# A graph-attention layer with gathers on GpSimd: every fourth gather waits until the last four have landed

## The reference

```python
Q, K, V = h @ Wq, h @ Wk, h @ Wv                      # 8 heads of 32
score = einsum(K[src], Q[dst]) / sqrt(32) + edge_bias # per edge and head
ex    = exp(score - segment_max(score, dst)[dst])
attn  = ex / segment_sum(ex, dst)[dst]
out   = segment_sum(attn * V[src], dst)               # then @ Wp + bp
```

## Time and profile before

| | |
|---|---|
| median of 3 runs (lowest to highest) | 5461.48 us (5446.13 to 5467.12) |
| the profiled execution: its time, its span | 5467.72 us, 5465.8 us |
| TensorE's mean granted clock over the span | 0.840 |
| busy: PE, DVE, ACT, POOL | 72%, 56%, 34%, 45% |
| first graph's edge pass, from its first gather to its last message product | 238.5 to 1899.0 us |
| in that pass, 238 to 1905 us: busy PE, DVE, ACT, POOL | 1180, 1288, 613, 964 us of 1667 |
| the same: granted clock, DMA engines' busy share, traffic | 0.86, 0.50, 142 GB/s |

### The profile page before, as it was taken

How to read it: one execution, slowest core, us unless ns; L and a number is a source line. 1 busy time by engine, 2 the same in 40 slices (tenths; PEclk the granted TensorE clock), 3 DMA queues, 4 the chain that set the end, 5 groups by cost and what they waited for, 6 DMA issues and landing times. The chain is left out here.

```text
span 5465.8 us, 69110 instructions
## 1 busy us (share of the span) xinstructions
PE 3936.6 (72%) x16154; PEld 2869.7 (53%) x16282; DVE 3067.4 (56%) x7623; ACT 1863.3 (34%) x5073; POOL 2451.9 (45%) x2442
## 2 busy tenths in 40 slices
PE   6867777767777659966953666666666328999999
PEld 4545545555555448866732444444444226777776
DVE  3277778877778775662063666666667773111111
ACT  1333333333333313311222444444445322333332
POOL 2256566666556360000166666666663321333332
PEclk8978888888888879987986767777777559999999
DMA  2545555555555332221173333333332360111111
GB/s 83 185 135 147 142 148 148 147 149 148 142 147 144 89 109 86 94 64 38 44 254 91 93 92 94 94 92 90 91 94 57 113 204 18 33 31 31 31 32 27
DMA packets 316126, 553.64 MB, mean 101 GB/s; under 512 B 63430, under 2 KB 213782, under 8 KB 315856
## 3 DMA queue, kind: packets, MB, share of 16 engines
q0 software_dynamic: 137120, 388.63, 26.6%
q1 hardware_dynamic: 178736, 161.98, 9.6%
HBM read 459.75 MB, written 90.62 MB: 101 GB/s over the span
## 5 line engine op out<-in xcount | busy, mean ns | idle before, releaser
L427 POOL DMA_INDIRECT attend_ring<-kv_rows,all_step_src x880 | 855.5, 972 | 669.8 <-PE attend_ps_agg L468 415.6
L927 POOL DMA_INDIRECT edge_ring<-head_rows,all_step_src x880 | 871.5, 990 | 485.9 <-issue 213.5
L963 PE MATMUL edge_ps_agg<-edge_msg,edge_sel 128*128 128x264 f32 x1760 | 670.7, 520 | 168.8 <-issue 67.9
L468 PE MATMUL attend_ps_agg<-attend_msg,attend_sel 128*128 128x264 f32 x1760 | 620.0, 456 | 179.3 <-DVE graph_qa L781 127.5
L963 PEld LDWEIGHTS edge_ps_agg<-edge_msg,edge_sel 128*128 128x128 f32 x1760 | 420.3, 259 | 292.6 <-issue 161.4
L452 PE MATMUL attend_ps_q<-graph_qa,attend_sel_t 128*128 x1760 | 538.9, 436 | 29.1 <-ACT attend_sel_t L577 23.2
L1256 DVE TENSOR_TENSOR graph_acc<-graph_acc,edge_ps_agg 128x264 f32 x880 | 369.5, 420 | 338.8 <-PE edge_ps_agg L963 166.2
L2811 DVE TENSOR_TENSOR moe_gl<-moe_ps_h,moe_act 128x341 f32<-128x341 f32 x210 | 107.9, 514 | 776.8 <-PE moe_ps_h L2729 776.8
L781 DVE SCALAR_TENSOR_TENSOR graph_qa<-graph_qa,all_step_same,attend_ps_agg 128x264 f32 x880 | 421.6, 479 | 190.8 <-remote 138.3
L468 PEld LDWEIGHTS attend_ps_agg<-attend_msg,attend_sel 128*128 128x128 f32 x1760 | 333.6, 213 | 350.9 <-issue 155.6
L2729 PE MATMUL moe_ps_h<-experts_w,moe_xt 128*128 x1680 | 501.8, 451 | 0.6 <-ACT moe_xt L2760 0.6
(11 more groups left out here) (424 smaller groups left out, 6404.4 us busy)
## 6 DMA issues: line engine op xcount, KB each, us to landing
attend_ring<-kv_rows,all_step_src POOLq DMA_INDIRECT x880
edge_ring<-head_rows,all_step_src POOLq DMA_INDIRECT x880
kv_rows<-qkv_kv SPq DMA_DIRECT2D x25, 512.0 KB, 3.0
experts_w<-in_w_t SPq DMA_DIRECT2D x16, 682.0 KB
attend_mask<-run_starts SPq DMA_DIRECT2D x440, 8.1 KB
edge_mask<-run_starts SPq DMA_DIRECT2D x440, 8.1 KB
head_rows<-hds_hh SPq DMA_DIRECT2D x25, 264.0 KB
qkv_x<-in_x SPq DMA_DIRECT2D x25, 256.0 KB, 3.2
```

What stands on the lines that cost most here:

```text
L427: nc.gpsimd.indirect_dma_start(ring[:, step % RING1, :], None, g.kv_rows, bass.IndirectOffsetOnAxis(g.step_src[:, step:step + 1], 0)).then ...
L468: nc.tensor.matmul(ps_agg[i % SUM_BANKS][:, 0:AGG], sel[:, q % 2, u % QU, :], msg[:, q % 2, u % QU, :], start=True, stop=True).then_inc(s_ ...
L927: nc.gpsimd.indirect_dma_start(ring[:, n % slots, u, :], None, g.head_rows, bass.IndirectOffsetOnAxis(g.step_src[:, step:step + 1], 0)).th ...
L963: nc.tensor.matmul(ps_agg[i % BANKS][:, 0:AGG], sel[:, q % 2, u % QU, :], msg[:, q % 2, u % QU, :], start=True, stop=True).then_inc(s_agg, 1)
```

## The change

The gather that opens a group of four steps, from step 44 on, waits for one more thing: that the group before it, whose four gathers were issued last, has landed in full. Group k has semaphore `landed[k % 11]`, which has reached 64 x (k // 11 + 1) by then.

```diff
                 if step >= RING1:
                     pool.wait_ge(s_agg, step - RING1 + 1)
+                    if step % QU == 0:
+                        before = step // QU - 1
+                        pool.wait_ge(landed[before % groups], (before // groups + 1) * (16 * QU))
                 nc.gpsimd.indirect_dma_start(ring[:, step % RING1, :], None, g.kv_rows,
                                              bass.IndirectOffsetOnAxis(g.step_src[:, step:step + 1], 0)
                                              ).then_inc(landed[step // QU % groups], 16)
```

## The result

| | before | with the change |
|---|---|---|
| runs, median (lowest to highest) | 5454.98 us (5446.13 to 5467.12, 4 runs) | 5682.66 us (5672.21 to 5683.9, 4 runs) |
| ratio, 95% interval | 1 | 1.0399 (1.0379 to 1.0418) |
| span of the profiled execution | 5465.8 us | 5682.0 us |
| granted clock over the span | 0.840 | 0.830 |

The change costs 228 us, where 48 were forecast and 5458 to 5555 us was the range. The direction was right, the size was not: it is nearly five times the forecast.

The account below looks back on a forecast made before the run. The edge pass's turn, 29.55 us, was taken as a loop through PE and DVE; POOL's 30.4 us cycle would replace it: 43 us over 51 turns, less 1.5, plus 6, +48, forecast 5510 us, range 5458 to 5555.

Parts of the forecast that it names:

- T: On POOL, time from the start of a group's last gather to the start of the next opener; forecast 3.8 us.
- The first piece: Transfer of a group's last gather, from its start to its last traffic: put at 3.2 us.
- The second piece: From a gather's last traffic to its semaphore, read from the expert pass's half-sized gathers: 0.3 us or slightly more.
- The third piece: Wake-up of POOL, read from a gather that waits for PE's sum: 0.27 us, taken as 0.3.
- The cycle: POOL's loop in a turn of the first graph's edge pass: four groups of 7.55 us plus slower gathers, 30.4 us.
- each 0.1 us of T is 20 us in all: Sensitivity once POOL is the bound: 0.1 us of T is 0.4 us a turn and 20 us in all.
- T = 4.3: Upper bound of the opener's delay, adding what a slow gather takes longer; 4.0 was used for the range's end.
- Hidden after all: Rival: POOL's idle 7.4 us a turn absorbs the waits if T is 3.6 or less; 5461 us, chance 0.20.
- The clock answers: Rival: PE, standing before step 12, falls to its lower clock more often; 5560 us, chance 0.14.
- Less crowding: Rival: gaps after four gathers let other transfers and POOL's descriptor writes run freer; 5435 us, faster, chance 0.04.
- products waiting for rows: Sign of being wrong: a product of line 676 waits for gathered rows; forecast said product reads are not hurt.
- A wait that is already met: Rival: all waits stand in the instruction order but may hold nothing back; left to the first rival, no own chance.

Follow-up runs that it names:

- e1: Changed kernel with the opener's two waits written in the other order, the landing's first, so the gather carries it: 5552.12 us, ratio 1.0169.
- e4: Changed kernel with three of the four openers of a turn waiting, all but that of step 4 of the 16: 5505.12 us, ratio 1.0084.
- e6: Changed kernel with the wait before every second gather instead of every fourth, for the one ahead of it, eight a turn: 6274.81 us in one run.
- e9: Changed kernel with waits only at steps 4 and 12 of the 16, on the chip where before takes 5018.7 us: 5187.91 us, ratio 1.0334.
- e10: Changed kernel with waits only at steps 0 and 8, the landing's written first, on the chip where before takes 5018.7 us: 5056.54 us, ratio 1.008.
- e8: Changed kernel with one wait a turn, at step 8 of the 16, on the chip where before takes 5018.7 us: 5015.31 us, ratio 0.9994.
- e2: Changed kernel with the opener waiting for the group before the last one, as many wait instructions: 5454.57 us, ratio 1.0009.
- e3: Changed kernel with only two of the four openers of a turn waiting, those of steps 0 and 8 of the 16: 5420.26 us, ratio 0.9925.
- e13: Changed kernel with waits only at steps 0 and 8 of the 16, run again in the fourth set: 5426.23 us, ratio 0.9949.

## Why the prediction was right in its direction and wrong in its size

- **The mechanism: right.** POOL turns from a follower of PE into the longest loop, the slack ahead of line 409 is used up, and each turn then lasts what POOL needs. PE waits for line 409 in 51 turns; groups of four stand 1.25 us apart with one T between; the kernels whose sum lies above the turn without waits (e1, e4, e6, e9, e10) have turns within 0.4 us of it.
- **The step that failed: T = 3.2 + 0.3 + 0.3 = 3.8 us.** It is 4.48. The first piece held. Windows at the end of a group's transfer in the changed kernel, whose last gather starts at 1019.00 (columns as in the earlier trace rows):

```profile
1022.00:1022.25 0.25, 0.25 (x3) 0.25 (x2) 0.00 (x0) 0.25 (x3) 0.00 (x0) 0.50 0.09 33
1022.25:1022.50 0.25, 0.25 (x3) 0.25 (x2) 0.00 (x0) 0.12 (x2) 0.00 (x0) 0.50 0.00 0
```

The traffic ends 3.0 to 3.25 us after the start, as forecast. The second piece was read from a transfer of half the size and is 0.5, not 0.3: e8's profile gives the landing times of these gathers,

```profile
DMA to landing us min/median/max: 3.2/3.7/5.4
```

and its median is 3.7 us. The third piece failed most. 0.27 us was the wake-up of a gather that carries its own wait (the view names DVE's line 768 for it, but the gather waits for PE's sum alone); here the landing's wait is an instruction of its own, and from the landing to the gather's start 4.48 - 3.7 = 0.8 us pass (0.76 by the semaphore records). e1 tests this piece by itself: carried by the gather, T is 3.93, which leaves 0.2 to 0.3 (0.26 by the records). The instruction order of the change shows the openers with two waits and the others with one; the prediction read that as one more condition at the old price.
- **Sum.** The cycle was put at 30.4 us and is 33.7. Of the 3.3 us, 4 x (4.48 - 3.8) = 2.7 are T, 0.3 the opener at place 4, whose landing comes 3.99 us after its gather's start in the trace, for a reason that stays open, and 0.3 the longer gathers, of whose 0.4 only half was taken and which are 0.5. The prediction's "each 0.1 us of T is 20 us in all" then gives the rest: 0.68 us are 139 us of the 180 that were missing, and the two small terms 30 more. The 11 that are left are about what the profiled execution of before, from which the prediction started, lay above the median of four (13 us).
- **The range: the upper end was the weak point.** T = 4.3 was worked out as the bound and cut to 4.0. Even 4.3 would have missed: it was built on a slow gather and kept 0.27 for the wake-up. No row of before had a gather behind two waits, and the bound had nothing for it.
- **The rivals.** "Hidden after all" needs T of at most 3.6 and falls. By the figure of the Trainium skill (DMA: Bandwidth & Descriptors, the section on the anatomy of one DMA), an estimate of 2.6 us for this transfer, it would have come true; the measured 3.7 us does not agree with it. "The clock answers" is seen (0.87 to 0.83) and costs nothing, since POOL's cycle covers it. "Less crowding" falls too: gathers take 979 ns in the mean, not less than the 972 of the earlier trace rows. One of the prediction's signs of being wrong, products waiting for rows, is there but small: 20.5 us in all, 26 times. "A wait that is already met" is e2, not the change.
- **A side that the prediction left out.** It gave a gain a chance of 4%, by less crowding. e3 and e13 show that two of these waits by themselves do gain on this kernel, 0.5 to 0.75%, for a reason that is open; with four of them any such gain is gone.

## What to carry to other kernels

An in-order queue that waits for the landing of its own last transfer turns latency into cycle time. Add up its cycle, (steps x spacing) + (waits x T), and set it against the turn: below, the waits are free, above, each costs all of T minus one spacing, every turn. T is start to landing plus the restart of the queue, and the restart has to be read at an instruction that waits in the same form: an opener behind two semaphores is not one behind a single semaphore. Where both are needed, let the DMA itself carry the wait that ends last, here the landing's, by writing it first: it was worth 130 us.

## What the runs showed of the hardware that was not expected

- A gather on POOL that carries its wait starts about 0.25 us after the landing (T 3.93 against a landing of 3.7); behind a separate wait instruction that is released at the same moment, about 0.75 us after it (T 4.48). The same separate wait, already met, adds nothing (e2: gathers 1.25 us apart).
- The landing of one 256 KB gather takes about as long behind one other (e6, T 4.3) as behind three (T 4.4 to 4.5).
- The same kernel has medians of 5451 to 5462 us on the other chips and 5018.7 us on another, 8% less, with a granted clock of 0.93 against 0.87 in this pass (e8 and before, 330 to 1600 us). Limits that depend on the length of a turn shift with it: e10's two waits, whose cycle adds up to 26.3 us, cost 0.8% there, while e3's two, with a cycle of 26.6 us, cost nothing at turns of 29 us.
